# Weighted values of the cross stage with the values as weights and a turn-back per pair of groups

## The reference, cut to what matters

```
xn = layer_norm(ctx, g1, b1);  ln_lat = layer_norm(layernorm(x), g2, b2)
q = ln_lat @ Wq;  k, v = split(concat([xn, ln_lat]) @ Wkv)
weight = einsum("bhld,bhnd->bhln", q * scale, k * scale)
weight = softmax(where(mask or latent key, weight, -big))
out = einsum("bhln,bhnd->bhld", weight, v)          # 16 heads, 256 queries, 64 columns
x = x + out.reshape(b, l, 1024) @ Wout
```

## Time and profile before

| | |
|---|---|
| median of 3 runs | 1055.75 us (1055.22 to 1056.27) |
| the profiled execution | 1054.65 us, its span on the core 1052.8 us |
| PE busy in the span | 1014.3 us (96%) |
| PEld busy | 943.1 us (90%) |
| DVE busy | 809.3 us (77%) |
| ACT busy | 666.8 us (63%) |
| POOL busy | 204.1 us (19%) |
| weighted values L303, PE | 1792 instructions, 215.2 us |
| exponentials L510, ACT | 512 instructions, 203.2 us |

### The profile page before, as it was taken

The page is one execution under the profiler, slowest core; times in us unless marked ns, Lnnn a source line. Parts: engine busy times, 40 slices in busy tenths (PEclk is TensorE's granted clock), DMA queues, the critical chain, the costliest instruction groups (busy, mean ns, idle before and its releaser), DMA issues. The chain is left out here.

```text
span 1052.8 us, 25657 instructions
## 1 busy us (share of the span) xinstructions
PE 1014.3 (96%) x8683; PEld 943.1 (90%) x8684; DVE 809.3 (77%) x3001; ACT 666.8 (63%) x1550; POOL 204.1 (19%) x265
## 2 busy tenths in 40 slices
PE   6999999999999999999999998988999999999997
PEld 6899999999999999999999998977888999889887
DVE  7887777685877786787787777579879889889753
ACT  4765565674665665566565566478776876767753
POOL 0111111110111111111111111342015203263213
PEclk9999999999999999999999999999999999999999
DMA  6000000000000000000000100520010000110000
GB/s 208 18 13 2 10 1 1 12 12 4 12 2 0 12 13 3 13 2 0 12 13 2 35 2 2 166 38 2 1 41 21 2 1 21 35 48 2 1 22 21
DMA packets 28803, 21.64 MB, mean 21 GB/s; under 512 B 12094, under 2 KB 26267, under 8 KB 28699
## 3 DMA queue, kind: packets, MB, share of 16 engines
q1 hardware_dynamic: 28529, 20.21, 6.5%
q10 hardware_dynamic: 170, 0.07, 0.0%
HBM read 19.17 MB, written 1.05 MB: 19 GB/s over the span
## 5 line engine op out<-in xcount | busy, mean ns | idle before, releaser
L303 PEld LDWEIGHTS pv_ps<-v,pt 128*128 128x128 f32 x1792 | 214.9, 192 | 9.3 <-issue 2.8
L303 PE MATMUL pv_ps<-v,pt 128*128 128x65 f32 x1792 | 215.2, 272 | 3.2 <-DVE o L818 1.8
L796 DVE CUSTOM_DVE_ANT_0 s_sb<-s_ps,pen,mstate 128x256 f32<-128x256 f32 (+1 forms) x512 | 199.9, 446 | 13.9 <-issue 11.0
L510 ACT ACTIVATE probs<-s_sb,mbias 128x256 f32<-128x256 f32 (+1 forms) x512 | 203.2, 470 | 0.0
L670 POOL TENSOR_TENSOR o<-o,alpha 128x260 f32<-128x260 f32 x128 | 85.7, 669 | 561.3 <-ACT alpha L504 561.3
L519 ACT ACTIVATE pt<-turn 128x512 f32<-128x512 f32 x128 | 76.2, 595 | 123.0 <-PE turn L290 109.1
L290 PE MATMUL turn<-ident,probs 128*128 128x128 f32 x896 | 123.8, 278 | 0.1
L290 PEld LDWEIGHTS turn<-ident,probs 128*128 128x128 f32 x896 | 98.8, 145 | 9.5 <-issue 0.3
L818 DVE TENSOR_TENSOR o<-o,pv_ps 128x260 f32<-128x260 f32 x128 | 53.9, 421 | 46.1 <-PE pv_ps L303 34.7
L279 PE MATMUL s_ps<-kh,qh 64*128 64x256 f32 (+1 forms) x512 | 78.9, 304 | 2.9 <-DVE x L840 1.6
L768 DVE TENSOR_TENSOR kl<-proj,kh 128x512 fp32r<-128x512 f32 (+1 forms) x63 | 41.3, 655 | 51.5 <-ACT kh L497 51.0
(11 more groups left out here) (432 smaller groups left out, 2730.7 us busy)
## 6 DMA issues: line engine op xcount, KB each, us to landing
raw<-in_ctx SPq DMA_DIRECT2D x24, 128.0 KB, 2.0
f_wqkv_raw<-in_L_ffn_wqkv SPq DMA_DIRECT2D x6, 512.0 KB, 5.3
f_w_raw<-in_L_ffn_w SPq DMA_DIRECT2D x8, 256.0 KB, 5.1
f_w_raw<-in_L_ffn_w SPq DMA_DIRECT2D x2, 640.0 KB
wkv_raw<-in_L_xattn_Wkv SPq DMA_DIRECT2D x1, 1024.0 KB, 8.5
wout_raw<-in_L_xattn_Wout SPq DMA_DIRECT2D x1, 1024.0 KB, 12.5
f_wo_raw<-in_L_ffn_wo SPq DMA_DIRECT2D x2, 512.0 KB, 4.7
x<-in_x SPq DMA_DIRECT2D x1, 768.0 KB, 9.6
```

What stands on the lines that cost most here:

```text
L303: last = pe.matmul(t.pv_ps[:, u, :], t.pt[g % 2][:, u, kt, :], t.v[:, kt, h, :], start=(kt == 0), stop=(kt == kts - 1))
L510: last = act.activation(t.probs[g % 2][:, u, 0:kts * P], t.s_sb[g % 2][:, u, 0:kts * P], ACT.Exp, bias=t.mbias[:, at:at + 1], scale=0.125)
L796: last = dve.tensor_tensor_reduce(out=t.s_sb[g % 2][:, u, 0:width], in0=t.s_ps[g % 2][:, u, 0:width], in1=t.pen[:, 0:width], scale=1.0, sc ...
```

## The change

The product of a group is turned round. The values become the weights: for each 128 keys and each of the two heads there is one matmul with 64 columns of values as weights and 256 columns of turned exponentials (both query blocks) as moving operand. The two heads write to the lower and the upper 64 partitions of `t.pv_ps`, which is now one bank [128, 2, 256] for two groups, an even and an odd one. The result has queries along the free axis; so ACT copies the bank to `t.ov` (`store_outputs`), PE turns it back with four 128x128 transposes (`turn_back`) into the same bank, and DVE adds both groups to the state at once (`add_outputs`).

The column of ones in `t.v` goes; the exponentials are summed on ACT by the instruction that makes them (`accum_out`), into `t.sums`, and POOL adds these sums to the 65th column of `t.o` with a second small instruction per group.

The order changes too. On PE the products of odd groups stand ahead of the projection, at even steps; those of even groups stay behind it, at odd steps; the turn-back stands at the head of the odd step. On ACT the copy to `t.ov` is the first thing of the odd step. On DVE the addition stands in the odd step behind the maxima. A product of an even group waits until the pair before has been added. Small buffers of the planning part are laid into others, and two semaphores are merged. In the diff `pair_at` gives a pair at odd steps j alone (the odd group j-4); the first use of it shown is PE's, the second ACT's.

```
+            def turn_back(m, g, kts):
+                pe.wait_ge(s["ov_stored"], 8 * m + g + 1)
+                for k in range(2):
+                    for qt in range(QT):
+                        last = pe.transpose(t.pv_ps[:, qt, k * P:(k + 1) * P], t.ov[:, k, qt * P:(qt + 1) * P], t.ident[:])
+                last.then_inc(s["o_turned_back"], 2)
...
             def weighted_values(m, g, kts):
...
-                if g or not isinstance(m, int):
+                if g % 2 == 0 and (g or not isinstance(m, int)):
                     pe.wait_ge(s["o_added"], 8 * m + g)
-                for u in range(GU):
-                    h = 2 * g + u // QT
-                    for kt in range(kts):
-                        last = pe.matmul(t.pv_ps[:, u, :], t.pt[g % 2][:, u, kt, :], t.v[:, kt, h, :],
+                for kt in range(kts):
+                    for o, rows in enumerate((slice(0, DH), slice(DH, P))):
+                        last = pe.matmul(t.pv_ps[rows, g % 2, :], t.v[:, kt, 2 * g + o, :], t.pt[g % 2][:, QT * o:QT * o + QT, kt, :],
                                          start=(kt == 0), stop=(kt == kts - 1))
...
+                    pair = pair_at(m, kind, prev, j)
+                    if pair:
+                        turn_back(*pair)
                     now = at_step(m, kind, prev, j - 2)
                     if now:
                         turn_probs(*now)
+                    now = at_step(m, kind, prev, j - 3)
+                    if now and j % 2 == 0:
+                        weighted_values(*now)
...
-                    if now:
+                    if now and j % 2:
                         weighted_values(*now)
...
                     last = act.activation(t.probs[g % 2][:, u, 0:kts * P], t.s_sb[g % 2][:, u, 0:kts * P], ACT.Exp,
-                                          bias=t.mbias[:, at:at + 1], scale=0.125)
+                                          bias=t.mbias[:, at:at + 1], scale=0.125, accum_out=t.sums[:, at:at + 1])
...
+            def store_outputs(m, g, kts):
+                act.wait_ge(s["pv_done"], 8 * m + g + 1)
+                if g >= 2 or not isinstance(m, int):
+                    act.wait_ge(s["o_turned_back"], 8 * m + g - 1)
+                act.activation(t.ov[:], t.pv_ps[:], ACT.Copy).then_inc(s["ov_stored"], 2)
...
                 for j in range(NG if kind else 6):
+                    pair = pair_at(m, kind, prev, j)
+                    if pair:
+                        store_outputs(*pair)
...
+                    pool.tensor_tensor(t.o[:, cols, DH], t.o[:, cols, DH], t.sums[:, cols], ALU.add).then_inc(s["rescaled"], 1)
...
+            def add_outputs(m, g, kts):
+                cols = slice(GU * (g - 1), GU * (g + 1))
+                dve.wait_ge(s["o_turned_back"], 8 * m + g + 1)
+                dve.wait_ge(s["rescaled"], 16 * m + 2 * g + 1)
+                added = t.o[:, cols, 0:DH].rearrange("p (h q) d -> p h q d", q=QT)
+                dve.tensor_tensor(added, added, t.pv_ps[:].rearrange("p q (h d) -> p h q d", d=DH), ALU.add).then_inc(s["o_added"], 2)
```

More of the change, by code:

```diff
@@ L159, in value_part @@
     def value_part(u):
-        return t.v[:, u % 2, (u // 2) * NG:(u // 2 + 1) * NG, 0:DH]
+        return t.v[:, u % 2, (u // 2) * NG:(u // 2 + 1) * NG, :]
     def load_norm(eng, which):
@@ L189, in at_step, with pair_at @@
         return None
+    def pair_at(m, kind, prev, j):
+        return at_step(m, kind, prev, j - 4) if j % 2 else None
     with nc.Block() as block:
@@ L465, in _ @@
             project_keys(0, KB)
-            pe.wait_ge(s["keys_spread"], 1)
-            pe.matmul(t.pv_ps[0:B, 1, 0:NCH + 1], t.row_of[:], t.listed[:], start=True, stop=True).then_inc(s["keys_listed"], 1)
+            pe.wait_ge(s["flags_ready"], 3)
+            pe.matmul(t.pv_ps[0:B, 1, 0:NCH + 1], t.row_of[:], t.listed[:], start=True, stop=True).then_inc(s["flags_ranked"], 1)
             pe.wait_ge(s["w_lo"], 3)
@@ L502, in softmax_part @@
                 if not isinstance(m, int):
-                    act.wait_ge(s["rescaled"], 8 * m + g - 7)
+                    act.wait_ge(s["rescaled"], 16 * m + 2 * g - 14)
                 act.activation(t.alpha[:, GU * g:GU * (g + 1)], t.mdiff[:, GU * g:GU * (g + 1)], ACT.Exp,
@@ L671, in body @@
                                        t.alpha[:, cols].unsqueeze(2).broadcast_to([P, GU, DH + 1]), ALU.mult).then_inc(s["rescaled"], 1)
+                    pool.wait_ge(s["rescaled"], 16 * m + 2 * g + 1)
+                    pool.wait_ge(s["p_ready"], 8 * m + g + 1)
+                    pool.tensor_tensor(t.o[:, cols, DH], t.o[:, cols, DH], t.sums[:, cols], ALU.add).then_inc(s["rescaled"], 1)
             pool.memset(t.o[:], 0.0).then_inc(s["state_zero"], 1)
@@ L679, in _ @@
             dve.memset(t.tick[:], 0.0).then_inc(s["s_read"], 2)
-            dve.memset(t.v[:, :, :, DH:DH + 1], 1.0).then_inc(s["x_added"], 2)
-            dve.memset(t.mask8[:, 1, :], 0)
+            dve.memset(t.mask8[:, 1, :], 0).then_inc(s["x_added"], 2)
             dve.memset(t.pen[:], 0.0).then_inc(s["pen_ready"], 1)
@@ L822, in normalise_output @@
                 dve.wait_ge(s["o_added"], 8 * m - 4 + 4 * half)
+                dve.wait_ge(s["rescaled"], 16 * m - 8 + 8 * half)
                 dve.reciprocal(t.inv[:, cols], t.o[:, cols, DH]).then_inc(s["inverse"], 1)
@@ L851, in body @@
                 for j in range(NG if kind else 6):
[L852 to L856, removed]
+                    if finish and j == 0:
+                        normalise_output(m, b, 0)
                     if kind and j == 4 and not final:
@@ L860, in body @@
                         maxima(m, j, KINDS[kind])
+                    pair = pair_at(m, kind, prev, j)
+                    if pair:
+                        add_outputs(*pair)
                     now = at_step(m, kind, prev, j - 2)
@@ L863, in body @@
                         store_turned(*now)
+                    if finish and j == 3:
+                        normalise_output(m, b, 1)
                     if finish and j in (1, 2, 4, 5):
@@ L950, in rank_flags @@
                 dve.tensor_scalar(t.listed[:, 0:NCH], t.key_row[:, 0:NCH], t.place[:], t.own_key[:], ALU.is_equal, ALU.mult
-                                  ).then_inc(s["keys_spread"], 1)
+                                  ).then_inc(s["flags_ready"], 1)
             twice, less = t.scratch[0:B, 0:ITEMS], t.scratch[0:B, ITEMS:ITEMS + NCH]
@@ L958, in plan_keys @@
                 dve.tensor_scalar(twice, t.iota[:], 2.0, None, ALU.mult)
-                dve.wait_ge(s["keys_listed"], 1)
+                dve.wait_ge(s["flags_ranked"], 2)
                 dve.tensor_copy(t.plan_rows[:, 0:NCH], t.pv_ps[0:B, 1, 0:NCH])
@@ L2548, in program @@
             t.mask_cols, t.listed, t.place = sb("mask_cols", [P, CH], U8), sb("listed", [P, NCH + 1]), sb("place", [P, 1])
-            t.key_row, t.key_col, t.own_key = sb("key_row", [P, P]), sb("key_col", [P, 1]), sb("own_key", [P, 1])
-            t.below, t.row_of = sb("below", [P, B, NCH]), sb("row_of", [P, B])
+            t.key_col, t.own_key = sb("key_col", [P, 1]), sb("own_key", [P, 1])
+            t.row_of = sb("row_of", [P, B])
             t.x_stats, t.x_mv = sb("x_stats", [P, TILES, 6]), sb("x_mv", [P, TILES, 2])
@@ L2562, in program @@
             t.kh, t.kl = (sb(n, [P, NG, KB], F32R) for n in ("kh", "kl"))
-            t.v = sb("v", [P, KT, H, DH + 1])
+            t.v = sb("v", [P, KT, H, DH])
+            t.ov = sb("ov", [P, 2, L])
             t.s_sb = [sb(f"s_sb{k}", [P, GU, KB]) for k in range(2)]
@@ L2566, in program @@
             t.pt = [sb(f"pt{k}", [P, GU, KT, P]) for k in range(2)]
-            t.mstate, t.mnew, t.mdiff, t.mbias, t.alpha, t.inv = (
-                sb(n, [P, H * QT]) for n in ("mstate", "mnew", "mdiff", "mbias", "alpha", "inv"))
+            t.mstate, t.mnew, t.mdiff, t.mbias, t.alpha, t.inv, t.sums = (
+                sb(n, [P, H * QT]) for n in ("mstate", "mnew", "mdiff", "mbias", "alpha", "inv", "sums"))
             t.o = sb("o", [P, H * QT, DH + 1])
             t.onorm = sb("onorm", [P, QT, H * DH])
+            t.key_row = t.onorm[:, 0, 0:P]
+            t.below = t.onorm[:, 1, 0:P].rearrange("p (b c) -> p b c", b=B)
             t.ot, t.ot_raw = split("ot", [P, 8, L])
@@ L2574, in program @@
             t.proj = ctx.enter_context(nc.psum_tensor("proj", [P, 512], F32))
-            t.pv_ps = ctx.enter_context(nc.psum_tensor("pv_ps", [P, GU, DH + 1], F32))
+            t.pv_ps = ctx.enter_context(nc.psum_tensor("pv_ps", [P, 2, L], F32))
             cross_stage(nc, t, sem_maker(ctx, "cross"), ahead, args)
```

9 lines of the change are left out of this document (2 added, 7 removed).

## The result

The changed kernel takes **1313.74 us** (median of 4 runs, 1311.89 to 1314.65) against 1055.49 of the kernel before beside it (1053.88 to 1056.27): ratio 1.2447, 95% interval 1.2425 to 1.2469. The forecast was 1329, range 1225 to 1410. The profiled execution took 1313.92 us, its span 1311.8.

The account below looks back on a forecast made before the run. PE was taken to bound the cross stage, working 618.8 of 625 us and never waiting. Waits 196, product -69, turn-back 27, changes of form 23 and clock 96 gave +273 on 1054.65: forecast 1329 us, range 1225 to 1410.

Parts of the forecast that it names:

- The new wait: Cross stage: PE's 64 turn-backs wait for ACT's copy to `ov` behind four exponentials, 3.48 us per wide step, +196 us.
- The clock: Cross stage: each of 64 PE waits brings a half-speed stretch losing 1.5 us, +96 us (ends 0 and 110).
- The rival in which the clock holds: Cross stage: PE's waits do not lower its clock, 1233 us (1302 or 1205 with other product cases); chance 0.19.
- The product: PE's product matmuls: the two heads overlap partly on column halves, 1.08 us per wide group instead of 1.73, -69 us.
- full overlap: Product: both column halves run entirely side by side, -97 us, total 1301 us; chance 0.08 with low clock.
- Changes of form: PE's array in the cross stage: three more switches per pair at 0.12 us, +23 us (0 to 38).
- Edits at nothing: POOL's small additions, the lost 65th column, memset and buffers, and even products' wait for DVE's addition: no cost.
- The rival on the other side: Turn-back: ACT's copy comes through before the projection ends and does not hold it, 1009 us; chance 0.02.
- own range 1290 to 1365: Range for the partial-overlap, low-clock case (1329 us, chance 0.44), from changes of form and the clock's ends.
- the 0.05 for the release: Turn-back wait: estimated 0.05 us for the release after ACT's copy to `ov`.
- 3.0 in step 6 of a half: Half items, step 6: estimated 3.0 us turn-back wait, as a copy of the next queries stands between.
- 1.5 behind the last item: Two turn-backs after the final item: estimated wait of 1.5 us each, 3 us together.

Follow-up runs that it names:

- run 3: Changed kernel with ACT's copy to `ov` moved to the even step, ahead of the projection's copy and the exponentials: 1147.70 us, ratio 1.0868.
- Run 4: Changed kernel with ACT's copy to `ov` in the even step and DVE's addition of both groups ahead of the odd step's maxima: 1054.57 us, ratio 1.001.
- Run 1: Changed kernel with twelve unused float32 matmuls put on PE ahead of the turn-back, at 63 of 64 places: 1237.26 us, ratio 1.1744.
- Run 2: Changed kernel with the product's two loops exchanged, all matmuls of one head before those of the other: 1310.78 us, ratio 1.2428.
- run 6: Run 4's kernel with DVE adding the finished result before the low parts of keys, and a half's step 3 turn-back behind the transposes: 1040.79 us, ratio 0.9868.
- run 7: Run 6's kernel with low parts of keys made from stored high parts (they come out zero), freeing the projection's bank after ACT's copy: 1038.07 us, ratio 0.9833.
- run 5: Run 4's kernel without `accum_out`, so the exponentials are not summed on ACT and denominators are left out: 1052.36 us, ratio 0.9973.

## Why the prediction was right, and where its sizes were off

- *The new wait.* Right in place and size: 3.37 us against 3.48 in a wide step, 189 against 196 in all; the 7 less lie in the latents items behind a half, 26 us for 32. Runs 3 and 4 show its worth: with ACT's copy moved and DVE's addition with it, 259 us go (1313.74 to 1054.57), waits and clock together.
- *The clock.* Right in kind, +105 for +96. Run 1 tells it from the wait, since it adds work and gains 76 us. The rival in which the clock holds (1233) is about where run 1 stands, by other means: there the waits are filled.
- *The product* is the step that was mis-sized: "written order lets only the second of one head run beside the first of the other". Run 2 shows that no such rule holds here; the term is -97 in place of -69, the end of the range that the forecast had given to full overlap (1301). The Trainium skill, "TensorEngine Tiling (Array Packing)", advises this exchange with two column tiles (section "Performance Considerations") and gives up to twice the speed for a dimension of at most 64 (section "Theoretical Speedup"); the trace agrees for the slots, four of 0.216 us where eight in a row would be 1.73.
- *Changes of form.* Entering column halves costs 0.09 (0.203 from the last transpose to the product's first matmul, 0.109 between transposes), and 0.05 more before the second pair of its matmuls; leaving them costs 0.10 at the first and 0.10 at the second matmul of the projection. A pair of groups enters them twice and has one leaving more than before: 2 x 0.14 + 0.20 = 0.48 us for the forecast 0.36, +31 in its bounds of 0 to 38.
- *Edits at nothing.* No wait of PE or DVE for POOL's small additions shows in the stage. The wait of even products for the addition is 0.6 us in the changed kernel, as said; run 3 shows that it is 68 as soon as PE comes on time. One wait was missed: DVE's addition of the finished result, +7.
- *The rival on the other side* (1009, if the copy did not hold the turn-back) was priced too low. Run 4 does what it asks for and takes 1054.6: about 45 us of it are lost, more than half of them to waits that were hidden before and to the clock behind them. PE now comes sooner, and the releases that follow the projection or the output projection have lost the product that stood over them. 14 of the 45 came back in run 6. Of the rest, run 7 shows 5.6 in the stage to be the bank; 8 are the changes of form at their measured price, 31 for 23; 4.1 are lost behind the stage; the waits of run 6 in and around the halves (the 4.0 and 3.2 us above; before, 1.8 for the addition) account for some 5. That leaves about 8 open.
- *The difference between forecast and result*, 1329 to 1314: the product is 28 and the waits are 7 us lower, the changes of form 8, the clock 9 and DVE's addition 7 higher, -11 in all; the other 4 are in the precision of the terms. The result came so near because these errors partly cancel, and that is luck.
- *In the forecast's working* the own range 1290 to 1365 does not follow from the ends that it names: 0 to 38 for the changes of form and 0 to 110 for the clock give 1210 to 1358. Three terms rest on no row: the 0.05 for the release, 3.0 in step 6 of a half, 1.5 behind the last item. They came out at 0.05 (446.50 + 0.58 to 447.13), 3.0, and 1.7 and 2.3.

## What to carry to other kernels

When an operand exchange puts a second engine's pass between two steps of the full engine, look first for what that second engine has written ahead of the pass: here four exponentials and a copy, 3.4 us for each wide pair. The full engine that was made to wait lost twice here, 189 us for the waits and 105 for the clock after them, so the order of the helpers was worth more than the 97 us that the product saved. And a product moved from behind a projection or copy takes its cover with it: list who was released under it before counting the gain.

## What was not expected of the hardware

Two column halves take plain float32 matmuls fully side by side (starts 6 ns apart), in either written order, 1310.78 and 1313.74 us. Matmuls that nobody uses made the kernel faster, 1237.26 against 1313.74, by the clock that they held. An exponential with its sum is followed by a read of 0.19 us on ACT, but in run 5 taking 512 of them out moved the time by 2.2 us, no more than the noise. Entering column halves and leaving them has a price, 0.14 and 0.20 us at full clock.
